# Two query groups and one key group change places in the hand-written order of an attention head loop

## The chip, the cores and the metric

The kernel runs on one core of a Trainium2 chip. The metric is the device time of one execution in microseconds (us). The core has five engines that run their own instruction streams in order and meet at semaphores: TensorE (PE, matmuls and transposes into PSUM), VectorE (DVE), ScalarE (ACT), GpSimd (POOL) and SyncE (SP, which issues DMAs). PE's clock is granted at one of two levels, 2.4 GHz (1.0 in the profile) or 1.2 GHz (0.5).

## The reference

A network of several layers on four images of 128 channels and 32 x 32 pixels: a non-local block and a mixture of convolutions, a causal attention, a feed-forward layer on the upper half of the tokens, an attention with three branches, and a mixture of experts. The change lies in the attention with three branches (16 heads of 64, 1024 tokens, batch 4). Cut to what matters:

```python
def _attn(q, k, v, mask=None):
    s = einsum('bhqd,bhkd->bhqk', q, k) / sqrt(64)
    return einsum('bhqk,bhkd->bhqd', softmax(where(mask, s, -1e9)), v)
o1 = _attn(q, k1, v1, causal)        # all earlier keys
o2 = _attn(q, ks, vs)                # 256 chosen tokens
o3 = _attn(q, kw, vw, winmask)       # the last 64 keys
o = g0 * o1 + g1 * o2 + g2 * o3      # gates, then a projection
```

q, ks and kw are each made of a plain half and a half that is rotated by position (rope).

## The kernel before, in words

stage_heads computes this attention in 16 passes (4 batches times 4 groups of 4 heads). Tokens are handled in groups of 256: the keys of the window are groups w0 to w3, the queries q0 to q3, the chosen keys s. Scores are computed twice: once with queries on partitions to find each query's maximum (near tiles for the window and the chosen keys, far tiles for all earlier keys), and once with keys on partitions, with the maxima subtracted in the same matmul, for the exponentials (score), the value products (value) and the denominators (add, sum). The numbers are kept in a high part rounded to fp32r and a low part, the rest.

A pass follows a list written out by hand, ORDER (L1971). Each engine walks through the whole list and does its share of each step. A step with a + belongs to the next pass and is done ahead, at the end of this one; the first such steps run once before the loop (the prologue, with clock-keeping matmuls between them), and the last pass has none. The steps that matter here:

- a.g: PE makes group g (L2388), ACT copies its plain half (L2572). rot.g: DVE multiplies the other half by the angles (L2656). rope.g: POOL adds the two products (L2327).
- tr.g: PE transposes the group with four transposes (L2398), ACT rounds it to its high part, with four copies for a query group and two for a key group (L2580). split.tr.g: DVE makes the low part with two instructions (L2674 for a query group, L2677 for a key group).
- near.i.n: PE makes a tile of scores of query tile i (L2430, and a mask at L2434 for the window keys), DVE takes its maxima (L2690). near.4.0 waits for split.tr.q2 and near.6.0 for split.tr.q3.
- v.x.n: PE makes values (L2416), ACT copies them (L2597). project.z: PE projects (L2517), DVE adds to the tokens (L2729).
- sum.z: PE makes denominators (L2510). norm.z: four DVE instructions in a row (L2714, L2716, L2718, L2722) turn, invert and apply them.
- double.w3: a DMA by SP, when tr.w3 is rounded. load.next: seven DMAs by SP for the next pass.

Two rules of the plan set most waits. The steps a, tr, k1, v, near and far ("filled" jobs, 97 in a pass) share PSUM banks 0 to 2, and each takes the next bank in the order of the list:

```python
self.bank = {key: n % 3 for n, (key, _) in enumerate(self.jobs)}
def bank_free(key, q):
    old = plan.before(plan.jobs, key, q, lambda other: plan.bank[other] == plan.bank[key])
    return old and (consumer[old[0]], ("split", *old) if old[0] in ("tr", "k1") else ("rot", old[1]) if old[0] == "a" else old)
```

plan.before finds the last job with the same bank, at need in the pass before. A job's matmuls thus wait for the last reader of that bank: the rotation of an a group, the split of a tr group or a key product, the copy of a v, the maxima of a near or far tile. The steps score, turn and sum share banks 3 to 5 in the same way.

At near.4.0 PE waits for its bank, issues nine matmuls whose result is overwritten (keep_clock(9, bank), L2426 and L2524), and only then waits for split.tr.q2.

Of the kernel before, what the change touches and what calls it, by code (L numbers as in the profile page):

```python
# [1968 lines left out]


ORDER = """  # L1971
wk tr.q2 tr.q3 split.tr.q2 split.tr.q3
score.4.0
score.4.1 v.v1.0 near.4.0
score.4.2
score.4.3
score.5.0 +load.next near.4.1 near.4.2 near.4.3
score.5.1 near.5.0
score.5.2
score.5.3 near.5.1 near.5.2 v.v1.1 near.5.3 near.6.0 value.4.4 near.6.1 near.6.2 near.6.3 turn.0.2 near.7.0 value.5.5 add.7 near.7.1 near.7.2 k1.0 near.7.3  # L1980
# [57 lines left out]
+score.1.1  # L2038
+score.2.0
+score.2.1  # L2040
+score.3.0 +rope.w3 +v.vw.1 +rope.q2 ysum.5 +v.vs.0 +tr.w3 +split.tr.w3 +a.q3 +rot.q3 +double.w3 project.5 +value.0.0 +value.1.1 +value.2.2 +add.0 +add.1 +value.3.3 +add.2 +add.3 +add.4 +add.5 +add.6 +sum.0 +rope.q3 +norm.0
"""


# [140 lines left out]
def stage_heads(nc, keep, PS, P, T, ident, identb, masks, turned, latents, d, slots, emptied):  # L2185
    with ExitStack() as ctx:
# [46 lines left out]
        def after(eng, q, at, *events):  # L2233


            values = {}
            for name, key in filter(None, events):
                value = plan.value(name, key, q, at)
                if value is not None:
                    values[name] = max(value, values.get(name, 0))  # L2240
            for name, value in values.items():
                eng.wait_ge(s[name], value if q is None else q * plan.a_pass(name) + value)
# [8 lines left out]
        def near_part(i, n):  # L2251

            if n < 2:
                return 1, KEEP3, 0
            return 2, 128 + REACH if i else 128, max(0, i * 128 - REACH)
# [5 lines left out]
        with nc.Block() as block:  # L2261
# [110 lines left out]
            def _(pe):  # L2372
# [4 lines that stand above are left out]
# [43 lines left out]
                def near_scores(key, q, at):  # L2420
                    _, i, n = key
                    made = {0: ("s", "w0", "q0"), 2: ("w1", "q1"), 4: ("q2",), 6: ("q3",)}[i] if n == 0 and i % 2 == 0 else ()
                    bank, x, w, c0 = ring(key), *near_part(i, n)
                    after(pe, q, at, bank_free(key, q))
                    if i == 4 and n == 0:
                        keep_clock(9, bank)  # L2426
                    after(pe, q, at, *(("reduced", ("split", "tr", g)) for g in made))
                    for m in range(2):
                        h = 2 * (n % 2) + m
                        last = nc.tensor.matmul(bank[:, m * w:(m + 1) * w], QH[:, h, i * 128:(i + 1) * 128], keys[x][:, h, c0:c0 + w],  # L2430
                                                start=m == 0, stop=x == 1 and m == 1)
                    if x == 2:
                        add = masks[:, 1:3, :].rearrange("p a n -> p (a n)")[:, 256 - w:]
                        last = nc.tensor.matmul(bank[:, 0:2 * w].rearrange("p (m w) -> p m w", m=2), identb[:, :],  # L2434
                                                add[:, None, :].broadcast_to([128, 2, w]), start=False, stop=True)
                    last.then_inc(s["filled"], 1)
# [84 lines left out]
                def keep_clock(count, bank=P[7]):  # L2521

                    for _ in range(count):
                        nc.tensor.matmul(bank[:, 0:384], identb[:, :], masks.rearrange("p a n -> p (a n)"), start=True, stop=True)  # L2524

                def one_pass(g, q):
                    for at, (ahead, *key) in enumerate(steps):
                        what, key = key[0], tuple(key)
                        if plan.left_out(q, ahead):
                            continue  # L2530
                        if q is None and what in ("a", "tr", "v", "near"):
                            keep_clock(2)
                        if what == "a":
                            group(key, q, at)
                        elif what == "tr":
                            turn_group(key, q, at)
                        elif what == "k1":
                            key_product(key, q, at)
                        elif what == "v":
                            value_product(key, q, at)  # L2540
                        elif what == "near":
                            near_scores(key, q, at)
                        elif what == "far":
                            far_scores(key, q, at)
                        elif what == "turn":
                            turn_maxima(key, q, at)
                        elif what == "score":
                            if q is None and key == ("score", 0, 0):
                                pe.wait_ge(s["rows"], 48)
                            key_major(key, q, at)  # L2550
                        elif what == "value":
                            values(key[1], key[2], q, at)
                        elif what == "sum":
                            denominators(key, q, at)
                        elif what == "project":
                            project(key[1], g, q, at)
# [327 lines left out]
```

## Time and profile before

| | us |
|---|---|
| three runs, median | 2646.47 |
| lowest, highest | 2644.33, 2648.10 |
| the profiled execution | 2643.02 |
| its span, first to last instruction | 2641.1 |

The head loop lies between 700 and 2400 us of the span. The profile is of one execution. Its page lists the busy time of each engine and the costliest groups of instructions; the trace behind it can be asked for a timeline of an engine, for the waits of an engine with what ended them, and for the busy time and the granted clock in any stretch. Times in a timeline are the start from the span's first instruction and the duration. Consecutive instructions of the same line and tiles are merged there into one row (x8: eight of them). The ends of matmuls are modelled, and a matmul may begin while the one ahead is still draining, so that starts are a better measure of PE than durations. What stands in brackets is the idle time of the engine before the row and what ended it.

### The profile page before, as it was taken

How to read it: one execution, taken by the hardware profiler on the slowest of the kernel's cores; microseconds unless marked ns; L12 is line 12 of the kernel's file. 1: busy time of each engine (PE TensorE's matmuls, PEld its weight loads, DVE VectorE, ACT ScalarE, POOL GpSimd, SP SyncE). 2: the span in 40 equal slices, each digit the busy share in tenths (PEclk: the TensorE clock that was granted, in tenths of full speed). 3: DMA queues.
4: the chain of work that ended last, by engine and by line, in shares of the span. 5: the costliest groups of instructions: out<-in, count | busy, mean ns of one | idle time of the engine just before them, and what ended most of it. 6: DMA issues, size and time to landing. Idle time of an engine off the chain costs nothing. (4 is left out here: it accounts for less than half of the span.)

```text
span 2641.1 us, 51557 instructions
## 1 busy us (share of the span) xinstructions
PE 2367.4 (90%) x16821; PEld 1718.4 (65%) x16821; DVE 1814.2 (69%) x3640; ACT 1413.0 (53%) x2489; POOL 1285.8 (49%) x972
## 2 busy tenths in 40 slices
PE   6889968666899999999999999999999999999767
PEld 4666645454667767677676676767667676675656
DVE  5868745585577686776867768676776867766436
ACT  2135544232565656656566565665657666575223
POOL 1016760000264746647365573755737557375445
PEclk8989988768999999999999999999999999999678
DMA  3040300013412111220212202122021220210233
GB/s 118 1 102 20 78 10 1 16 50 87 129 43 54 28 41 36 49 54 16 54 36 45 58 16 54 36 45 58 16 54 36 45 58 16 54 20 17 70 118 102
DMA packets 82189, 128.14 MB, mean 49 GB/s; under 512 B 15824, under 2 KB 58240, under 8 KB 81728
## 3 DMA queue, kind: packets, MB, share of 16 engines
q1 hardware_dynamic: 77616, 119.47, 17.9%
q0 software_dynamic: 3024, 7.43, 0.9%
q8 instruction: 46, 0.75, 0.1%
q10 hardware_dynamic: 1472, 0.24, 0.1%
q14 instruction: 31, 0.25, 0.0%
HBM read 61.26 MB, written 20.79 MB: 31 GB/s over the span
## 5 line engine op out<-in xcount | busy, mean ns | idle before, releaser
L2621 ACT ACTIVATE a_PT<-PS 128x512 f32<-128x512 f32 (+1 forms) x1104 | 584.4, 565 | 365.1 <-PE PS L2486 241.4
L2339 POOL TENSOR_TENSOR a_KT<-a_PT 128x256 f32<-128x256 f32 (+2 forms) x176 | 354.3, 2025 | 459.7 <-ACT a_PT L2621 451.2
L2339 POOL TENSOR_TENSOR a_KT<-a_KT,a_PT 128x2048 f32<-128x2048 f32 (+3 forms) x128 | 391.8, 3061 | 10.3 <-ACT a_PT L2621 1.0
L2690 DVE TENSOR_REDUCE a_NM<-PS 128x2 fp32r<-128x512 f32 (+2 forms) x512 | 290.8, 612 | 134.2 <-PE PS L2430 73.5
L2480 PE MATMUL PS<-a_QH,a_K 128*128 128x512 f32 (+3 forms) x768 | 293.1, 392 | 2.9 <-ACT a_PT L2621 2.8
L2702 DVE TENSOR_REDUCE a_MX<-PS 128x1 f32<-128x512 f32 (+3 forms) x432 | 265.6, 664 | 32.7 <-PE PS L2445 18.1
L2480 PE MATMUL PS<-a_QH,a_KSW 128*128 128x192 f32 (+3 forms) x832 | 264.5, 339 | 12.1 <-DVE a_NM L2690 10.5
L2445 PE MATMUL PS<-a_K,a_QH 128*128 128x512 f32 (+3 forms) x768 | 252.3, 404 | 9.4 <-DVE a_K L2677 8.1
L2481 PE MATMUL PS<-a_QL,a_K1B 76*128 76x512 f32 (+3 forms) x768 | 260.1, 349 | 0.0
L2430 PE MATMUL PS<-a_KSW,a_QH 128*128 128x256 f32 (+2 forms) x1024 | 198.8, 306 | 4.1 <-DVE a_QL L2674 4.1
L2430 PEld LDWEIGHTS PS<-a_KSW,a_QH 128*128 128x128 f32 x1024 | 164.0, 193 | 49.6 <-DVE a_NM L2690 19.5
L2327 POOL TENSOR_TENSOR a_TM<-a_R 128x128 f32<-128x128 f32 x288 | 124.1, 458 | 130.0 <-DVE a_R L2656 130.0
L2480 PEld LDWEIGHTS PS<-a_QH,a_KSW 128*128 128x128 f32 x832 | 160.4, 193 | 41.3 <-issue 13.5
L2677 DVE TENSOR_TENSOR a_KSW<-PS,a_KSW 64x512 fp32r<-64x512 f32 x160 | 110.3, 689 | 108.3 <-ACT a_KSW L2580 105.3
L2580 ACT ACTIVATE a_QH<-PS 64x512 fp32r<-64x512 f32 x256 | 151.5, 592 | 51.3 <-PE PS L2398 46.6
L2486 PE MATMUL PS<-masks,identb 128*128 128x128 bf16 (+3 forms) x592 | 172.2, 291 | 0.0
L2480 PEld LDWEIGHTS PS<-a_QH,a_K 128*128 128x128 f32 x768 | 149.0, 194 | 33.6 <-issue 14.5
L2445 PEld LDWEIGHTS PS<-a_K,a_QH 128*128 128x128 f32 x768 | 135.6, 193 | 45.5 <-DVE a_MX L2702 17.3
L2607 ACT ACTIVATE a_QL<-PS 12x1024 fp32r<-12x1024 f32 x128 | 130.1, 1017 | 60.7 <-PE PS L2460 58.3
L2481 PEld LDWEIGHTS PS<-a_QL,a_K1B 76*128 76x128 f32 x768 | 147.1, 192 | 9.6
L2656 DVE TENSOR_TENSOR a_R<-PS,a_angles 128x512 f32<-128x512 f32 x144 | 96.2, 687 | 72.9 <-ACT a_TM L2572 71.9
L2481 PE MATMUL PS<-a_QL,a_KWB 76*128 76x192 f32 (+2 forms) x576 | 141.1, 275 | 0.0
(434 smaller groups left out, 5223.2 us busy)
## 6 DMA issues: line engine op xcount, KB each, us to landing
a_KWB<-a_KSW SPq DMA_DIRECT2D x64, 256.0 KB, 3.3
a_K1B<-a_K SPq DMA_DIRECT2D x32, 512.0 KB, 4.9
a_XC<-latents SPq DMA_DIRECT2D x16, 512.0 KB, 3.8
a_CKS<-latents SPq DMA_DIRECT2D x16, 512.0 KB, 4.6
a_CF<-latents SPq DMA_DIRECT2D x16, 448.0 KB, 4.2
slots<-in_empty_slots SPq DMA_DIRECT2D x1, 5160.0 KB, 18.7
f_XB<-slots SPq DMA_DIRECT2D x8, 645.0 KB, 6.0
c_EX<-in_experts SPq DMA_DIRECT2D x1, 4608.0 KB, 18.0
```

The source lines that it names most:

```text
L2327: last = nc.gpsimd.tensor_tensor(TM[:, x, :, 32 + c:48 + c], r[:, :, 0, c:c + 16], r[:, :, 1, other:other + 16], ALU.add)
L2339: nc.gpsimd.tensor_tensor(total, one_in, other_in, ALU.add).then_inc(s["added"], 1)
L2430: last = nc.tensor.matmul(bank[:, m * w:(m + 1) * w], QH[:, h, i * 128:(i + 1) * 128], keys[x][:, h, c0:c0 + w], start=m == 0, stop=x == 1 ...
L2445: last = nc.tensor.matmul(bank[:, m * w:(m + 1) * w], QH[:, h0 + m, i * 128:(i + 1) * 128], K1[:, h0 + m, c0:c0 + w], start=m == 0, stop=n ...
L2480: nc.tensor.matmul(out, keys[x][:, h, c:c + 128], QH[:, h, start:start + w], start=m == 0, stop=False)
L2481: last = nc.tensor.matmul(out, upper[x][0:DH + ROWS, h, c:c + 128], QL[0:DH + ROWS, h, start:start + w], start=False, stop=mask is None an ...
L2486: last = nc.tensor.matmul(by_heads[:, :, 0:cols], identb[:, :], add[:, None, :].broadcast_to([128, each, cols]), start=False, stop=True)
L2580: last = nc.scalar.activation(odd_even({"q": QH, "w": KW, "s": KS}[g[0]], e, rows, tokens(g)), ring(key)[e * DH:(e + 1) * DH, :].rearrange ...
L2607: nc.scalar.activation(QL[DH:DH + ROWS, :, p * PAIR:(p + 1) * PAIR], turning(key)[DH:DH + ROWS, None, 0:PAIR].broadcast_to([ROWS, QUAD, PA ...
L2621: nc.scalar.activation(PT[:, to:to + width], turning(key)[:, 0:width], ACT.Exp).then_inc(s["taken"], 1)
L2690: nc.vector.tensor_reduce(NM[:, i, DH:].rearrange("p (h x) -> p h x", x=3)[:, h:h + 2, x], ring(key)[:, 0:2 * w].rearrange("p (h n) -> p h ...
L2702: nc.vector.tensor_reduce(out, ring(key)[:, 0:heads * w].rearrange("p (h n) -> p h n", h=heads), AX.X, ALU.max, negate=True).then_inc(s["r ...
```

## The change

tr.q3 with its split moves from the start of a pass to behind near.4.3. tr.q2 with its split moves from the start of a pass to the end of the pass before, ahead of tr.w3; project.5 moves ahead of both. split.tr.w3, rot.q3 and rope.q3 move behind norm.0, in this order. The nine clock-keeping matmuls at near.4.0 go.

```diff
 ORDER = """
-wk tr.q2 tr.q3 split.tr.q2 split.tr.q3
+wk
 score.4.0
 score.4.1 v.v1.0 near.4.0
 score.4.2
 score.4.3
-score.5.0 +load.next near.4.1 near.4.2 near.4.3
+score.5.0 +load.next near.4.1 near.4.2 near.4.3 tr.q3 split.tr.q3
 score.5.1 near.5.0
 score.5.2
 score.5.3 near.5.1 near.5.2 v.v1.1 near.5.3 near.6.0 value.4.4 ...
...
-+score.3.0 +rope.w3 +v.vw.1 +rope.q2 ysum.5 +v.vs.0 +tr.w3 +split.tr.w3 +a.q3 +rot.q3 +double.w3 project.5 +value.0.0 +value.1.1 +value.2.2 +add.0 +add.1 +value.3.3 +add.2 +add.3 +add.4 +add.5 +add.6 +sum.0 +rope.q3 +norm.0
++score.3.0 +rope.w3 +v.vw.1 +rope.q2 ysum.5 +v.vs.0 project.5 +tr.q2 +split.tr.q2 +tr.w3 +a.q3 +double.w3 +value.0.0 +value.1.1 +value.2.2 +add.0 +add.1 +value.3.3 +add.2 +add.3 +add.4 +add.5 +add.6 +sum.0 +norm.0 +split.tr.w3 +rot.q3 +rope.q3
...
                     after(pe, q, at, bank_free(key, q))
-                    if i == 4 and n == 0:
-                        keep_clock(9, bank)
                     after(pe, q, at, *(("reduced", ("split", "tr", g)) for g in made))
```

## Rows read from the trace of the kernel before

**Rows 1.** The page, busy time, share of the span and instructions of each engine

```profile
PE 2367.4 (90%) x16821; PEld 1718.4 (65%) x16821; DVE 1814.2 (69%) x3640; ACT 1413.0 (53%) x2489; POOL 1285.8 (49%) x972
```

**Rows 2.** Windows of two passes: length, busy time by engine (instructions), granted clock, DMA

```profile
927.02:1039.40 112.38, 108.75 (x793) 78.08 (x793) 80.67 (x136) 70.72 (x127) 65.22 (x50) 0.98 0.17 41
...
1482.29:1593.01 110.72, 107.16 (x793) 77.27 (x793) 80.65 (x136) 70.50 (x127) 65.20 (x50) 1.00 0.18 41
```

**Rows 3.** Waits of PE from 816 to 2380: total us, times, longest

```profile
PE PS L2524 <- DVE a_QL L2674: 24.7, 15, 1.7
```

**Rows 4.** Timeline of PE around the head of a pass: start, duration, line, tiles

```profile
1472.98 0.60 PE L2398 MATMUL PS<-ident,a_TM 128*128 128x128 f32 x4
1473.47 1.13 PE L2388 MATMUL PS<-a_WQ,a_CF 112*128 112x256 f32 x4
1474.44 1.05 PE L2517 MATMUL PS<-a_WP,a_YT 128*128 x8
...
1476.72 1.06 PE L2510 MATMUL PS<-a_KT,a_ones 128*32 128x512 f32 x8
1477.71 1.09 PE L2398 MATMUL PS<-ident,a_TM 128*128 128x128 f32 x8
1478.56 0.48 PE L2480 MATMUL PS<-a_QH,a_KSW 128*128 128x512 f32 x1
...
1479.58 1.06 PE L2416 MATMUL PS<-a_WV,a_CF 112*128 112x128 f32 x8
1482.29 1.64 PE L2524 MATMUL PS<-masks,identb 128*128 128x384 bf16 x9 [1.66 <-DVE a_QL L2674]
1483.63 0.54 PE L2430 MATMUL PS<-a_KSW,a_QH 128*128 128x256 f32 x2
...
1485.41 0.60 PE L2430 MATMUL PS<-a_KSW,a_QH 128*128 128x256 f32 x4
...
1486.28 0.53 PE L2480 MATMUL PS<-a_QH,a_KSW 128*128 128x512 f32 x1
...
1488.04 0.60 PE L2430 MATMUL PS<-a_KSW,a_QH 128*128 128x256 f32 x4
...
1488.66 1.06 PE L2416 MATMUL PS<-a_WV,a_CF 112*128 112x128 f32 x8
```

**Rows 5.** Timeline of DVE in the same stretch

```profile
1474.90 1.39 DVE L2677 TENSOR_TENSOR a_KSW<-PS,a_KSW 64x512 fp32r<-64x512 f32 x2 [4.58 <-ACT a_KSW L2580]
1476.32 0.69 DVE L2656 TENSOR_TENSOR a_R<-PS,a_angles 128x512 f32<-128x512 f32 x1
...
1477.93 0.72 DVE L2714 STREAM_TRANSPOSE a_RT<-PS 128x512 f32<-128x512 f32 x1 [0.33 <-PE PS L2510]
...
1479.81 0.69 DVE L2722 TENSOR_TENSOR a_YA<-PS,a_RT 128x512 f32<-128x512 f32 x1
...
1480.85 1.39 DVE L2674 SCALAR_TENSOR_TENSOR a_QL<-PS,a_QH 64x512 fp32r<-64x512 f32 x2
...
1485.85 2.22 DVE L2690 TENSOR_REDUCE a_NM<-PS 128x2 fp32r<-128x512 f32 x4 [0.47 <-PE PS L2430]
```

**Rows 6.** Timeline of ACT in the same stretch

```profile
1478.41 4.83 ACT L2580 ACTIVATE a_QH<-PS 64x512 fp32r<-64x512 f32 x8 [2.83 <-PE PS L2398]
```

**Rows 7.** Timeline of POOL in the same stretch

```profile
1470.56 1.27 POOL L2348 TENSOR_TENSOR a_YT<-a_YA,a_YB 128x512 f32<-128x512 f32 x1 [2.51 <-DVE a_YB L2722]
```

**Rows 8.** Windows of two long idle times of PE in earlier stages and behind them

```profile
264.67:267.78 3.11, 0.00 (x1) 0.01 (x1) 3.11 (x5) 0.60 (x1) 2.82 (x3) 1.00 0.92 207
267.78:271.20 3.42, 3.42 (x17) 3.19 (x17) 1.37 (x4) 1.89 (x4) 2.17 (x2) 0.57 0.88 200
...
448.46:452.73 4.27, 0.00 (x1) 0.00 (x1) 3.08 (x23) 1.30 (x3) 0.00 (x0) 0.99 0.00 0
...
452.73:459.40 6.67, 6.67 (x41) 4.27 (x42) 3.77 (x9) 2.25 (x3) 0.00 (x0) 0.50 0.00 0
```

**Rows 9.** Timeline of PE at the start of the loop's first pass

```profile
700.83 0.43 PE L2398 MATMUL PS<-ident,a_TM 128*128 128x128 f32 x2 [2.77 <-DMA a_WP<-in_w_proj]
```

## The prediction

> **What bounds the kernel now.** The page comes first: TensorE (PE) is busy for 90% of the span, the next engine for 69% [rows 1]. The windows of single passes come next: a pass of the head loop, from one filler burst to the next, is 110.72 us, and PE is busy in 107.16 of them at full clock [rows 2]. The loop runs 16 passes. PE sets the pass, so each microsecond added to PE's order or taken from it counts 15 times, and once more, differently, in the first pass. The waits of PE over the loop say what is left to win: the longest, 24.7 us in 15 waits, is for the low parts that VectorE (DVE) makes at L2674 [rows 3], and the timeline shows where: nine fillers start at 1482.29 after 1.66 us of idling, and near.4.0 follows at 1483.63 [rows 4]. The spot that the change rewrites thus costs 1.66 + 1.34 = 3.0 us of a pass. Behind it PE runs without a gap as far as these rows go; a PE that comes out of this spot later is not given the time back.
>
> **The bank ring, which decides this.** Every "filled" job (a, tr, k1, v, near, far) takes the next of three PSUM banks in the order of the text, and its matmuls wait until the reader of the bank's last job is done. A pass has 97 such jobs, 3 x 32 + 1, so the first job of a pass takes the same bank as the last job of the pass before. Before, the first is tr.q2 and the last a.q3, whose reader rot.q3 is long done: DVE runs it at 1476.32 and PE needs it at 1477.71 [rows 4, 5]. After, the first is v.v1.0 and the last still a.q3, so v.v1.0 waits for rot.q3, and the change puts rot.q3 on DVE behind norm.0 and split.tr.w3. Counting on: near.4.0 gets tr.q2's bank, near.4.1 tr.w3's, tr.q3 near.4.1's, near.5.2 tr.q3's, v.v1.1 near.5.0's.
>
> **Part 1: the end of a pass on PE.** Times are those of the pass shown, in us past 1400. From tr.w3 (72.98) to sum.0 (76.72) PE does tr.w3, a.q3, project.5 and four value products [rows 4]. After, the same work stands there in another order, with tr.q2 added: 0.49 (one tr group, 72.98 to 73.47). sum.0 starts at 77.21 and, 0.99 long as before (76.72 to 77.71), gives way to score.4.0 at 78.20, where that had 78.56, since both groups are gone from there. project.5 can go first: its input is ready at 71.83 (70.56 + 1.27 on POOL [rows 7]). It is 1.05 long, so tr.q2 starts at about 74.0. PE wants v.v1.0 1.02 after score.4.0 (78.56 to 79.58), at 79.22.
>
> **Part 2: the same stretch on ScalarE (ACT) and DVE.** A q group is rounded by four copies; eight take 4.83, so four 2.42 and the two of tr.w3 1.2; they start 0.70 after the transposes (77.71 to 78.41) [rows 4, 6]. ACT rounds tr.q2 from 74.7 to 77.1 and tr.w3 to 78.3. DVE runs split.tr.q2 (1.39) to 78.5. norm.0 can start 1.21 after sum.0 (76.72 to 77.93), at 78.42, so it starts at 78.5 and takes 2.57 (77.93 to 79.81 + 0.69): 81.07. Then split.tr.w3, 1.39, and rot.q3, 0.69: 83.1 [rows 5]. PE goes on 0.05 after such a release (80.85 + 1.39 to 82.29): v.v1.0 at 83.15. **That is a wait of 3.9 us**, some 3.8 of it idle. v.v1.0 is 1.06 long, of which some 0.9 pass before the next job starts, so near.4.0, whose split is done long before, starts at about 84.0 where it had 83.63. The old wait and the fillers are gone, a longer wait has come: +0.4 in all.
>
> **Part 3: tr.q3 in its new place.** From near.4.0 to near.4.1 are 1.78 (83.63 to 85.41), then three near tiles take 0.87 (to 86.28) [rows 4]: PE is ready for tr.q3 at 86.65. Its bank is free when DVE has reduced near.4.1, which starts 0.44 after that tile does (85.41 to 85.85) and takes about 0.7 [rows 4, 5]: PE at 86.95, another 0.3. rope.q3, which DVE's rot.q3 releases at 83.1, has 3.5 us for two instructions on a POOL with nothing else to do. With 0.5 for tr.q3 itself score.5.1 starts at 87.45 where it had 86.28. Then ACT rounds q3 from 87.65 to 90.05, with the exponentials of score.5.1 to 5.3 queued behind, and DVE splits it to 91.45, with the maxima of near.5.0 and 5.1 queued behind. PE has near.5.1 at 89.2 (1.76 after score.5.1, 86.28 to 88.04) and would have near.5.2 some 0.25 later, but its bank is tr.q3's: 91.5. **A second wait, 2.1 us, some 1.9 idle.** v.v1.1 then waits for the maximum of near.5.0, 0.7 behind the split: 92.15 where it had 88.66. That is **+3.5 us a pass**; from there the order is as before.
>
> **Part 4: the clock.** In most passes PE stays at 2.4 GHz after the 1.66 us wait. In the one from 927.02 the grant falls, 0.98 in the mean, and it takes 112.38 instead of 110.72 [rows 2]: a fall costs 1.66 us. It is one of two such passes; the other 13 of those 15 waits leave the clock alone. Longer idling does not: after 3.11 us the grant was 0.57 over 3.42 us, after 4.27 us 0.50 over 6.67 us with PE busy throughout [rows 8]. 3.8 us lies between these two. I take a fall in nearly each pass at 1.5 us (1.66, less a part of the slow stretch that lies under the wait), bounds 0 and 3.0, the latter half of 6.67 less the end that the second wait hides. The second wait, 1.9 us idle, is nearest to the 1.66 us ones; between 2 in 15 there and every time at 3.11, I take 4 in 10 at 1.5: 0.6 a pass, bounds 0 and 1.66.
> The Trainium skill (TensorE: Matmul & The Clock Gate, section "A second HAM failure mode: psum-queue depth-cycling") speaks more strongly against such an order: it says that a PE which idles briefly between groups of matmuls as it cycles through PSUM banks keeps dropping to the slow clock and back. By that rule both waits would end in a fall in every pass, rival 2's time instead of the sum below; 13 of the 15 waits of 1.66 us do not bear it out.
>
> **What costs nothing.** double.w3 is issued when tr.w3 is rounded, 78.3, some 3.4 us later than now (ACT releases split.tr.w3 for 74.90 [rows 5]); the first score that reads it, score.7.0, has all of the near tiles 5 to 7 and four key products ahead of it. SP's seven loads for the next pass stand behind double.w3 in its queue; nothing reads them before a.s, behind score.13.1, half a pass on. Without that cover a pass would lose those 3.4 us. tr.q2's copies overwrite what score.24 read last, which PE issues ahead of tr.q2. score.4.2 needs norm.0's first transpose only, done at 79.2.
>
> **The first pass.** The load of WP stands on SP behind double.w3, and PE waits 2.77 us for WP, until 700.83 [rows 9]. q2's four copies now go ahead of tr.w3's on ACT, 2.4 us, and WP lands that much later. In return most of v.v1.0's wait passes under that one. With the 3.1 us of part 3 this pass loses about 3 us (0 to 6).
>
> **The sum**, against the profiled execution (2643.02 us; span 2641.1): 15 x 3.5 = 52.5, the first pass 3, the two falls of before gone -3.3, new falls 15 x (1.5 + 0.6) = 31.5, in all +83.7, so 2726.7 or **2727 us**. The median of the runs shown is 3.4 above the profiled one; the sum does not move for that.
>
> **Rivals.**
> 1. No low clock after either wait: 2643.0 + 52.5 + 3 - 3.3 = 2695. For it: 13 of 15 waits of before; against it: the rows at 3.11 and 4.27 us. 0.08.
> 2. Both waits end in a fall every time: 15 x (3.5 + 3.32) + 3 - 3.3 = 102, so 2745; with the first slow stretch twice as long 15 x (3.5 + 3.0 + 0.6) + 3 - 3.3 = 106, 2749. For it: the long idle rows; against it: 13 of 15. 0.10.
> 3. Not slower: rot.q3 is not what v.v1.0 waits for in the end. The point is 79.22: with rot.q3 done by then v.v1.0 goes at once, near.4.0 at 80.1, and near.4.1, held by split.tr.w3 (82.4), at 82.45, 3.3 sooner than in my sum (85.8). All behind it moves along: 3.5 - 3.3 = 0.2 a pass, and 2643.0 + 3 + 3 - 3.3 = 2646, no change. For it: the 3.0 us of wait and fillers do go. Against it: the ring as counted, and a DVE chain of 2.57 + 1.39 + 0.69 behind sum.0 with 1.0 us of PE work beside it. 0.05.
> 4. Faster: as 3, with split.tr.w3 and q3's rounding hidden too. Then the 3.0 us come out in full: 2643 - 45 = 2598. ACT and DVE would have to do 2.42 + 1.39 beside the 2.5 us that PE has from tr.q3 to near.5.2. 0.04.
> The forecast keeps 0.73. A measurement of this kernel can tell about 0.2%, 5 us, from no change. Faster 0.04, same 0.05, slower 0.91. The range goes from rival 1 to rival 2 with some room: 2692 to 2752.
>
> **What would show it.** No fillers at near.4.0. PE waiting at the value product (L2416) for DVE's rotation (L2656), some 3.8 us, 15 times; PE waiting at a near tile (L2430) for L2674, some 1.9 us, 15 times. Passes of 114.2 us at full clock, 116 to 117 with falls, and a granted clock clearly below 1.00 over the loop. The forecast is wrong if v.v1.0 starts within 1 us of score.4.1's end, or if near.5.2 does not wait.

## The result, and the profile after

The changed kernel takes 2753.12 us (median of four runs, 2752.69 to 2754.90) where the kernel before takes 2645.65 beside it (2644.33 to 2648.10): a ratio of 1.0411, 95% interval 1.0397 to 1.0425, slower by 4.1%. The forecast was 2727 in 2692 to 2752: the right sign and the right waits, 26 us too little, and the time lies 1 us above the range. Behind the removed lines the line numbers fall by two: the wait for L2674 of before is one for L2672 here, the rotation is L2654.

The page of after, busy time, share and instructions of each engine (against [rows 1]): PE has 39 us more of busy time with 142 matmuls fewer, so its matmuls became slower.

```profile
PE 2406.6 (87%) x16679; PEld 1741.3 (63%) x16679; DVE 1816.6 (66%) x3640; ACT 1419.2 (52%) x2489; POOL 1286.2 (47%) x972
```

Waits of PE in the loop of after, 820 to 2490 us: total, times, longest (against [rows 3]). The one wait of 1.7 us has become three.

```profile
PE PS L2416 <- DVE a_R L2654: 48.9, 15, 3.3
PE PS L2428 <- DVE a_QL L2672: 30.6, 15, 2.0
...
PE PS L2478 <- DVE a_RT L2712: 7.1, 14, 0.5
```

Windows of after: a pass from score.4.0 to score.4.0, four stretches of it, and the pass behind it: length, busy time by engine (instructions), granted clock, DMA (against [rows 2]). From the fourth pass on, passes of 118.5 and 117.1 us alternate; the second kind lacks the second slow stretch. In the stretches from 1528.13 and from 1541.78 PE runs at 1.2 GHz.

```profile
1524.38:1642.84 118.46, 110.57 (x788) 79.10 (x784) 80.78 (x137) 70.95 (x127) 65.26 (x50) 0.96 0.17 39
...
1524.38:1528.13 3.75, 1.46 (x8) 0.60 (x4) 3.49 (x6) 2.10 (x5) 0.00 (x0) 1.00 0.56 134
1528.13:1534.95 6.82, 5.34 (x19) 4.76 (x20) 2.40 (x4) 1.97 (x4) 0.97 (x2) 0.50 0.48 126
1534.95:1541.78 6.83, 4.68 (x29) 3.70 (x29) 4.34 (x8) 4.46 (x8) 1.03 (x1) 1.00 0.00 0
1541.78:1545.19 3.41, 3.41 (x19) 1.98 (x17) 1.57 (x3) 0.69 (x1) 3.41 (x1) 0.50 0.00 0
...
1642.84:1759.94 117.10, 109.25 (x788) 78.67 (x784) 80.93 (x137) 70.95 (x127) 65.31 (x50) 0.97 0.17 39
```

Timeline of PE in after at the head of that pass: start, duration, line, tiles, and in brackets the idle time before and what ended it (against [rows 4]). sum.0, score.4.0, score.4.1, v.v1.0, near.4.0, near.4.1, tr.q3, near.5.2, v.v1.1:

```profile
1523.41 1.04 PE L2508 MATMUL PS<-a_KT,a_ones 128*32 128x512 f32 x8
1524.38 0.50 PE L2478 MATMUL PS<-a_QH,a_KSW 128*128 128x512 f32 x1
...
1525.62 0.50 PE L2478 MATMUL PS<-a_QH,a_KSW 128*128 128x512 f32 x1 [0.51 <-DVE a_RT L2712]
...
1529.61 2.08 PE L2416 MATMUL PS<-a_WV,a_CF 112*128 112x128 f32 x8 [3.27 <-DVE a_R L2654]
1531.34 0.78 PE L2428 MATMUL PS<-a_KSW,a_QH 128*128 128x256 f32 x2
...
1534.47 0.82 PE L2428 MATMUL PS<-a_KSW,a_QH 128*128 128x256 f32 x4
...
1535.88 0.66 PE L2398 MATMUL PS<-ident,a_TM 128*128 128x128 f32 x4
...
1540.46 0.47 PE L2428 MATMUL PS<-a_KSW,a_QH 128*128 128x192 f32 x2 [2.04 <-DVE a_QL L2672]
...
1541.18 1.56 PE L2416 MATMUL PS<-a_WV,a_CF 112*128 112x128 f32 x8
```

Timeline of DVE in after (against [rows 5]): split.tr.q2, norm.0's first and last instruction, split.tr.w3, rot.q3, one behind the other without a gap, as counted beforehand:

```profile
1523.43 1.39 DVE L2672 SCALAR_TENSOR_TENSOR a_QL<-PS,a_QH 64x512 fp32r<-64x512 f32 x2 [2.04 <-ACT a_QH L2578]
1524.85 0.72 DVE L2712 STREAM_TRANSPOSE a_RT<-PS 128x512 f32<-128x512 f32 x1
...
1526.72 0.69 DVE L2720 TENSOR_TENSOR a_YA<-PS,a_RT 128x512 f32<-128x512 f32 x1
1527.44 1.39 DVE L2675 TENSOR_TENSOR a_KSW<-PS,a_KSW 64x512 fp32r<-64x512 f32 x2
1528.87 0.69 DVE L2654 TENSOR_TENSOR a_R<-PS,a_angles 128x512 f32<-128x512 f32 x1
```

Timeline of PE in after, the first pass (against [rows 9]): the wait for WP is 3.93 us and ends at 703.06, 2.2 later than before.

```profile
703.06 0.79 PE L2478 MATMUL PS<-a_QH,a_KSW 128*128 128x512 f32 x1 [3.93 <-DMA a_WP<-in_w_proj]
```

### The profile page after: what moved, and what is told of

It reads as the page before. It is cut to its first block and busy times, and to the rows that moved or that the text cites. A ratio compares the mean times of both kernels' runs of the same rounds, so it can differ in the third digit from the quotient of the medians.

```text
span 2750.6 us, 51259 instructions
## 1 busy us (share of the span) xinstructions
PE 2406.6 (87%) x16679; PEld 1741.3 (63%) x16679; DVE 1816.6 (66%) x3640; ACT 1419.2 (52%) x2489; POOL 1286.2 (47%) x972
## 5 line engine op out<-in xcount | busy, mean ns | idle before, releaser
L2478 PE MATMUL PS<-a_QH,a_KSW 128*128 128x192 f32 (+3 forms) x832 | 276.4, 353 | 23.7 <-DVE a_NM L2688 10.5
L2428 PE MATMUL PS<-a_KSW,a_QH 128*128 128x256 f32 (+2 forms) x1024 | 218.5, 326 | 36.7 <-DVE a_QL L2672 36.7
L2428 PEld LDWEIGHTS PS<-a_KSW,a_QH 128*128 128x128 f32 x1024 | 180.5, 212 | 90.9 <-DVE a_QL L2672 40.7
L2478 PEld LDWEIGHTS PS<-a_QH,a_KSW 128*128 128x128 f32 x832 | 166.5, 200 | 73.9 <-issue 30.9
L2654 DVE TENSOR_TENSOR a_R<-PS,a_angles 128x512 f32<-128x512 f32 x144 | 96.3, 687 | 72.9 <-ACT a_TM L2570 71.9
L2672 DVE SCALAR_TENSOR_TENSOR a_QL<-PS,a_QH 64x512 fp32r<-64x512 f32 x128 | 87.9, 687 | 80.6 <-ACT a_QH L2578 78.7
```

What stands on the lines that cost most here:

```text
L2478: nc.tensor.matmul(out, keys[x][:, h, c:c + 128], QH[:, h, start:start + w], start=m == 0, stop=False)
```

## The experiments

What is told apart is how much of the loss is the order alone and how much the clock, which part of the order makes the first wait, and what the removed matmuls had been doing. All kernels compute the whole result. Ratios are to the kernel before, run beside each; the "theory" of an expectation is what was held when it was written, and it changes on the way.

**The order with the clock held.** Fillers go into both waits, to banks whose readers are done.

```diff
+                    if (kind, x) == ("v1", 0):
+                        after(pe, q, at, bank_free(("near", 4, 0), q))
+                        keep_clock(18, ring(("near", 4, 0)))
...
+                    if (i, n) == (5, 2):
+                        after(pe, q, at, ("residual", ("project", 5)))
+                        keep_clock(11)
```

> The changed kernel with clock-keeping matmuls placed inside its two new waits: 18 ahead of v.v1.0, into the bank that near.4.0 overwrites afterwards, and 11 ahead of near.5.2, into the bank that value.4.4 overwrites. At 0.15 us each they take 2.7 and 1.65 us, less than the waits, so the order of the work and the waits stay. If the two waits cost 3.5 us a pass at full speed and all the rest of the loss is TensorE's clock, the grant stays near 1.00, passes take 114.2 to 115 us, and the kernel takes about 2643 + 15 x 3.5 + 3 = 2700 us (2695 to 2712). If the waits themselves cost 7 us a pass and the low clock falls into idle time, it stays at 2745 to 2755.

2703.89 us, ratio 1.0225 (1.0208 to 1.0242). Behind the first its passes are all alike, at full clock; the window of one:

```profile
1506.48:1620.90 114.42, 111.25 (x814) 78.79 (x812) 80.80 (x137) 70.85 (x127) 65.30 (x50) 1.00 0.17 40
```

What is left of the two waits that were filled (waits of PE, 820 to 2440 us):

```profile
PE PS L2419 <- DVE a_R L2660: 4.8, 15, 0.4
PE PS L2434 <- DVE a_QL L2678: 3.6, 15, 0.2
```

So the order costs 114.42 - 110.72 = 3.7 us a pass (3.5 in the forecast), and over half of the loss. The rest, 1.0411 against 1.0225, is the clock: 49 us where the forecast had 31.5.

**Only the first wait held.** The same without the eleven fillers at near.5.2.

> The changed kernel with the 18 clock-keeping matmuls ahead of v.v1.0 alone; the second wait, at near.5.2, idles as in the change. The order alone cost 60 us with both waits filled (2704). Theory (each wait's own idle time decides, and some 2 us at near.5.2 fell in 5 to 6 of 16 passes where tr.q3 alone was moved): 2704 + 6 x 1.6 = 2714 (2706 to 2720), so that the first wait's falls are worth some 40 of the 49 us that the clock cost, 2.6 each. Rival (with no low stretch behind the first wait, the second falls every time): 2704 + 15 x 1.6 = 2728 or more.

2727.94 us, ratio 1.0324 (1.0307 to 1.0342): the rival. One pass of it, and the slow stretch in it; the grant falls in each of the 15 passes behind the first one, after an idle time of 2.0 us:

```profile
1515.20:1631.18 115.98, 111.05 (x803) 78.56 (x801) 80.81 (x137) 70.87 (x127) 65.22 (x50) 0.99 0.17 40
1529.79:1533.20 3.41, 3.41 (x18) 1.78 (x16) 1.47 (x3) 0.69 (x1) 3.39 (x1) 0.50 0.00 0
```

A fall here costs 115.98 - 114.42 = 1.56 us a pass. In after the grant falls at this wait in 9 of the 15 passes only (from the fourth on in every second). Holding the first wait thus takes one slow stretch away and brings the other into every pass, and the 25 us between the two kernels are less than the first stretch is worth: passes of 117.1 with that stretch alone stand 2.7 above 114.42, and the second stretch adds 1.35 where it comes.

**norm.0 last.** split.tr.w3, rot.q3 and rope.q3 ahead of norm.0, the rest as in after.

```diff
-... +sum.0 +norm.0 +split.tr.w3 +rot.q3 +rope.q3
+... +sum.0 +split.tr.w3 +rot.q3 +rope.q3 +norm.0
```

> The changed kernel with norm.0 put back behind split.tr.w3, rot.q3 and rope.q3 (that part of the change undone). Theory, the chain norm.0, split.tr.w3, rot.q3 on VectorE holds v.v1.0: rot.q3 is done 2.6 us sooner, but score.4.1 now waits for the first transpose of norm.0, behind them, some 2.6 us, so v.v1.0 comes about 1.3 us sooner than in the changed kernel, and the clock still falls: 2753 - 15 x 1.3 = 2733 us (2715 to 2740). Rival, the order on VectorE is not what holds TensorE: 2753.

2726.13 us, ratio 1.0306 (1.0289 to 1.0323), as expected. The profile is of the longest of its five executions, 2739.41. Waits of PE, 820 to 2450 us:

```profile
PE PS L2478 <- DVE a_RT L2712: 35.4, 14, 2.5
PE PS L2428 <- DVE a_QL L2672: 28.6, 14, 2.0
```

v.v1.0 no longer waits for the rotation; in its place score.4.1 waits 2.53 us for norm.0. Which of the two stands last on DVE chooses who waits, and it changes the size: 2.53 us of idling for 3.78, and the slow stretch behind it is 3.41 us long in each of the 15 passes behind the first, where in after it is 6.83 in 14 of 15. The window of one such stretch:

```profile
1530.75:1534.16 3.41, 3.41 (x13) 2.94 (x12) 1.71 (x3) 1.81 (x4) 0.00 (x0) 0.50 0.68 223
```

**Another bank for v.v1.0.** The ring is shifted by one bank for the jobs at the head of a pass, so that v.v1.0 takes the bank of tr.q2 and not of a.q3.

```diff
-        self.bank = {key: n % 3 for n, (key, _) in enumerate(self.jobs)}
+        self.bank = {key: (n + (n < 78)) % 3 for n, (key, _) in enumerate(self.jobs)}
```

> The changed kernel with the bank ring turned by one for the first 78 jobs of a pass, so that v.v1.0 takes the bank of tr.q2 in place of that of a.q3; nothing else. Theory, the bank of a.q3 makes the first wait: TensorE no longer waits for the rotation at v.v1.0; near.4.0, which now has the bank of tr.w3, waits for split.tr.w3 instead, 1.7 us, and starts 1.6 us sooner than in the changed kernel. Idle times are then below 2.1 us and the clock falls in fewer passes: 2643 + 15 x (3.5 - 1.6) + 3 = 2675 at full clock, 2675 to 2705 with falls. Rival, the ring does not matter: 2753.

2720.69 us, ratio 1.0298 (1.0271 to 1.0326): the wait for the rotation is gone, which shows that the bank had made it, but the time is 16 us above the expected range. Waits of PE, 820 to 2450 us:

```profile
PE PS L2428 <- DVE a_QL L2672: 30.1, 15, 2.1
PE PS L2428 <- DVE a_KSW L2675: 24.6, 15, 1.7
```

The window of a pass:

```profile
1512.81:1626.92 114.11, 107.82 (x785) 77.50 (x783) 80.88 (x137) 70.94 (x127) 65.32 (x50) 0.99 0.17 40
```

near.4.0 now waits 1.7 us for split.tr.w3, about as long as it had in [rows 3], and yet one or two slow stretches fall in every pass (114.1 to 116.6 us). That spoke against the reading that 1.66 us of idling leaves the clock alone, and led to the kernel without fillers, below.

**tr.q3 alone.** The kernel before, nine fillers kept, with tr.q3 and its split behind near.4.3.

```diff
-wk tr.q2 tr.q3 split.tr.q2 split.tr.q3
+wk tr.q2 split.tr.q2
...
-score.5.0 +load.next near.4.1 near.4.2 near.4.3
+score.5.0 +load.next near.4.1 near.4.2 near.4.3 tr.q3 split.tr.q3
```

> The kernel before with tr.q3 and its split moved behind near.4.3 and nothing else changed (fillers kept). The fillers then stand in a bank that is free, so they run inside the wait for split.tr.q2 and near.4.0 starts some 1.3 us sooner; tr.q3 in its new place costs 0.8 us and the wait at near.5.2 and v.v1.1 2.7 us. Theory: +2.2 us a pass, 2643 + 33 = 2676 us, and up to 2690 if the clock falls behind the second wait in half of the passes. Rival, tr.q3's place costs nothing and the loss all comes from the first wait: 2625, faster than before.

2682.97 us, ratio 1.0156 (1.0134 to 1.0177), as expected. Two passes, without and with a fall, which comes behind the 2.0 us wait at near.5.2 (in 6 of the 15 passes behind the first):

```profile
1495.22:1607.92 112.70, 108.09 (x794) 77.17 (x793) 80.70 (x136) 70.60 (x126) 65.22 (x51) 1.00 0.18 41
1946.02:2060.23 114.21, 109.59 (x794) 77.78 (x793) 80.69 (x137) 70.59 (x126) 65.25 (x51) 0.99 0.17 40
```

This part of the change alone costs 2.0 us a pass at full clock. That is a net figure: with tr.q3 gone from the ring ahead of it, near.4.0's bank is free sooner, the fillers run inside the first wait, and near.4.0 comes 4.17 us behind score.4.0 where it came 5.07 behind it in before.

**Before without its fillers.**

```diff
-                    if i == 4 and n == 0:
-                        keep_clock(9, bank)
```

> The kernel before without its nine clock-keeping matmuls at near.4.0, nothing else. They stand behind PE's wait for its bank and end 1.34 us behind the release by split.tr.q2 (1482.29 to 1483.63 in the trace of before), so without them near.4.0 starts 1.34 us sooner; part of this is given back at score.4.3, which needs a bank whose exponential ACT has not done by then. Theory (the clock follows the idle time, and 1.66 to 2.0 us of it leave the grant alone in most passes): passes of about 110.2 us, a fall in a third of them at most, 2632 to 2645. Rival (the fillers are what keeps the clock at full speed): the grant falls in every pass, 15 x 1.66 = 25 us more, 2655 to 2670.

2658.56 us (2644.70 to 2671.23), ratio 1.0054 (1.0024 to 1.0085): the theory that held up to here fell. Three passes:

```profile
1599.15:1711.79 112.64, 109.00 (x785) 78.70 (x784) 80.98 (x136) 70.54 (x126) 65.15 (x51) 0.97 0.18 41
1937.10:2047.39 110.29, 105.97 (x785) 76.22 (x784) 80.68 (x137) 70.39 (x126) 65.22 (x51) 1.00 0.18 42
2047.39:2159.22 111.83, 107.48 (x785) 77.49 (x784) 80.97 (x136) 70.40 (x126) 65.21 (x51) 0.98 0.18 41
```

At full clock the order is indeed worth 0.43 us a pass (110.72 to 110.29). But the grant falls in 12 of 15 passes, in eight of them for twice as long as in the others, against 2 of 15 with the fillers, behind the same idle time of 1.7 us. So the nine matmuls that followed that idle time in before did matter. One long fall and one short one, near.4.0 and the slow stretch of each, and a fall of before:

```profile
1603.59 0.77 PE L2428 MATMUL PS<-a_KSW,a_QH 128*128 128x256 f32 x2 [1.70 <-DVE a_QL L2672]
1603.50:1610.33 6.83, 6.74 (x21) 5.48 (x22) 3.88 (x6) 4.54 (x9) 0.00 (x0) 0.50 0.00 0
...
2051.83 0.47 PE L2428 MATMUL PS<-a_KSW,a_QH 128*128 128x256 f32 x2 [1.75 <-DVE a_QL L2672]
2054.06:2057.47 3.41, 3.41 (x14) 2.94 (x13) 2.55 (x5) 1.78 (x4) 0.00 (x0) 0.50 0.00 0
...
927.06:930.47 3.41, 3.41 (x12) 2.07 (x13) 1.38 (x2) 2.56 (x5) 0.00 (x0) 0.50 0.00 0
```

The fillers are no plain guard against a fall, though. In the eight long ones the slow stretch starts within 0.1 us of the wait's end, and in both falls of before close to it too (0.04 and 0.11 us behind it): with the nine fillers it lasts 3.41 us, without them 6.83. In the other four it starts 1.9 to 2.7 us behind the wait's end, and before has no fall of that kind. The eight follow one another, each in a pass of 112.6 to 112.7 us, so the 12 are not 12 separate chances. A pass without fillers is also 0.43 us shorter at full clock; whether that alone moves the falls was not tried.

**Before with its fillers inside the wait.** Eleven to bank 7 ahead of the wait, in place of nine behind it.

```diff
                     if i == 4 and n == 0:
+                        after(pe, q, at, ("residual", ("project", 5)))
+                        keep_clock(11)
+                    after(pe, q, at, bank_free(key, q))
-                        keep_clock(9, bank)
```

> The kernel before with its clock-keeping matmuls put into the wait instead of behind it: eleven of them go to bank 7, free since project.5, ahead of PE's wait for split.tr.q2 at near.4.0, in place of the nine behind that wait. Theory (what holds the clock is that PE works during the 1.66 us, and the 1.34 us behind the wait are then saved): passes of 110.3 us as without fillers, and no fall, 2643 - 15 x 0.42 - 3.3 = 2633 (2628 to 2640). Rival (the fillers hold the clock only behind the wait): falls as in e4_no_fillers, 2650 to 2665.

2634.73 us, ratio 0.9963 (0.9948 to 0.9979), as expected. The window of a pass:

```profile
1472.33:1582.58 110.25, 107.72 (x796) 77.20 (x795) 80.69 (x136) 70.42 (x126) 65.17 (x51) 1.00 0.18 42
```

PE's timeline at near.4.0, the fillers and the near tile:

```profile
1474.86 1.95 PE L2525 MATMUL PS<-masks,identb 128*128 128x384 bf16 x11
1476.77 0.48 PE L2431 MATMUL PS<-a_KSW,a_QH 128*128 128x256 f32 x2
```

No pass but the first has a slow stretch, and near.4.0 follows the fillers at once. Placed in the wait, fillers cost nothing; placed behind it, they held near.4.0 up by 1.34 us. Part of that is made up at score.4.3, where PE waits 0.58 us without the delay, and 0.47 us a pass is left (110.72 to 110.25).

**The next pass's work in DVE's idle time.** An order that follows from this: tr.q2 with its split, v.v1.0, the near.4 tiles and near.5.0 of the next pass at the end of a pass, where DVE idled 4.58 us [rows 5]; sum.0 and norm.0 to the head, behind score.4.1; tr.q3 behind near.5.2; no fillers.

```diff
-wk tr.q2 tr.q3 split.tr.q2 split.tr.q3
 score.4.0
-score.4.1 v.v1.0 near.4.0
-score.4.2
+score.4.1 near.5.1 near.5.2 tr.q3 sum.0 norm.0
+score.4.2 split.tr.q3 near.5.3
...
+score.21.3 +near.1.2 +rope.w2 +tr.w2 +rope.q1 +wk +double.w1 ...
...
++score.2.1 +split.tr.q2 +rot.q3
++score.3.0 +split.tr.w3 ysum.5 +near.4.0 project.5 +v.vs.0 +near.4.1 +near.4.2 ...
```

> An order of my own that follows from the diagnosis: no clock-keeping matmuls; tr.q2 with its split, v.v1.0, the four near.4 tiles and near.5.0 of the next pass stand at the end of a pass, where DVE idles 4.58 us ahead of split.tr.w3 in the kernel before; sum.0 and norm.0 move behind score.4.1, tr.q3 behind near.5.2, so that no wait of PE has norm.0, a split and a rotation in a row ahead of it. Theory (the 1.66 us wait and the 1.34 us of fillers both leave the path, and no new wait comes for the low parts of q2): 15 x 3.0 to 15 x 3.9 us less, 2585 to 2605, PE without a wait over 1 us for L2674's line. Rival (the wait only moves, to the rounding of tr.q2 and tr.w3 at the pass's end or to the split of q3 at near.6.0): 2640 or more.

2653.42 us (2631.66 to 2665.22), ratio 1.0037 (1.0010 to 1.0064): the gain did not come. The waits at the head are gone, but PE waits 1.70 us elsewhere, at near.2.0, and in the profiled execution, one of 2644.95, the grant falls there in 8 of 15 passes. PE's timeline at near.2.0:

```profile
1565.78 0.74 PE L2427 MATMUL PS<-a_KSW,a_QH 128*128 128x256 f32 x4 [1.70 <-DVE a_QL L2671]
```

DVE's timeline, the subtraction of wk ahead of it:

```profile
1559.16 2.65 DVE L2679 TENSOR_TENSOR a_WKL<-a_WK,a_WKH 64x256 fp32r<-64x256 f32 x1 [1.41 <-ACT a_WKH L2599]
```

POOL's timeline, the addition that runs at that time:

```profile
1556.98 4.55 POOL L2338 TENSOR_TENSOR a_KT<-a_KT,a_PT 128x2048 f32<-128x2048 f32 x1
```

The subtraction of wk takes 2.65 us here, 0.41 in before, and it ends 0.28 after the addition that POOL had begun ahead of it (1559.16 + 2.65 = 1561.81, against 1556.98 + 4.55 = 1561.53). The split of q1, which near.2.0 needs, stands behind it.

**wk beside an idle POOL.** The same order with wk behind split.tr.q3.

```diff
-score.4.2 split.tr.q3 near.5.3
+score.4.2 split.tr.q3 wk near.5.3
...
-score.21.3 +near.1.2 +rope.w2 +tr.w2 +rope.q1 +wk +double.w1 ...
+score.21.3 +near.1.2 +rope.w2 +tr.w2 +rope.q1 +double.w1 ...
```

> The order of e6_ahead with one step put elsewhere: wk (the split of the key projection's weight into a high and a low part) goes from behind rope.q1, near the end of a pass, to behind split.tr.q3. In e6_ahead its subtraction on DVE, with both inputs in SBUF, took 2.65 us there, beside POOL additions that follow one another without a gap (4 in 17.44 us), against 0.41 us in the kernel before beside an idle POOL; the split of q1 stood behind it and PE waited 1.70 us for that at near.2.0, 15 times. Theory (POOL's running addition holds the subtraction up): it takes 0.4 us again, no wait over 0.8 us is left in the loop, the clock does not fall, passes of 108.0 us, 2600 (2592 to 2612). Rival (the length comes from elsewhere, or the wait goes to another place): passes of 109.5 us or more, 2625 to 2655.

2595.42 us, ratio 0.9821 (0.9787 to 0.9856): the theory, and 1.8% faster than the kernel before. The two longest waits of PE, 820 to 2360 us:

```profile
PE PS L2477 <- DVE a_NM L2687: 9.8, 15, 0.7
PE PS L2442 <- DVE a_K L2674: 7.4, 15, 0.5
```

The window of a pass:

```profile
1459.39:1567.17 107.78, 106.41 (x784) 76.11 (x784) 80.79 (x137) 70.05 (x127) 65.21 (x50) 1.00 0.18 42
```

DVE's timeline, the subtraction of wk:

```profile
1463.18 0.41 DVE L2679 TENSOR_TENSOR a_WKL<-a_WK,a_WKH 64x256 fp32r<-64x256 f32 x1
```

No wait of PE over 0.7 us is left in the loop, no slow stretch either, and a pass is 2.94 us shorter than in [rows 2], about the 3.0 us that the wait and the fillers had cost there.

## Why the prediction was right in kind and short in size

- **The bank ring held.** v.v1.0 waits for rot.q3 in all 15 passes, 3.27 us, and 0.51 at score.4.1 ahead of it makes 3.78, where 3.8 was forecast. Moving one bank removes that wait. The 0.51 was not foreseen: the forecast let only score.4.2 depend on norm.0's first transpose, and it is score.4.1. It cost nothing, since it lies inside the time to rot.q3.
- **Parts 1 and 2 held.** From score.4.0 to v.v1.0 are 5.23 us (1524.38 to 1529.61); the forecast had 4.95. near.4.0 then follows after 1.73, not 0.9, for the clock is already low.
- **Part 3 held.** near.5.2 idles 2.04 us (1.9 forecast), and the order costs 3.7 us a pass at full clock (3.5).
- **Part 4 failed, in the term of the first fall.** It took 1.5 us a pass, with 3.0 as its upper bound. The slow stretch is 6.82 us, of which 1.5 lie under the wait and PE works 5.34 [the window from 1528.13]; work at half speed loses half of that, 2.67 us, and the passes with this stretch alone are 2.7 longer. The idle time, 3.8 us, lay between the two rows of [rows 8], whose slow stretches are 3.42 and 6.67 us, and the forecast took its price from the pass at 927.02, where a wait of 1.66 us was followed by a stretch of 3.41. That is 1.2 us in 15 passes, 18 of the 26 us.
- **The second fall was right in the mean by luck.** 1.35 us in about every second pass is some 0.7; the forecast had 4 in 10 at 1.5, 0.6. But its row, 13 of 15 waits of 1.66 us that left the clock alone, said nothing of a wait without fillers: take them away and 12 of 15 fall. The sum that put the fillers down as 1.34 us of pure cost, and the use of 13 of 15 against rival 2, both fall with it: taking the fillers out alone won 0.43 us a pass at full clock and lost more than that to the clock.
- **The first pass** starts 1.4 us later (703.06 for 701.67) and lasts 114.34 for 110.91: 4.8 in all, 3 forecast (0 to 6). With 0.2 a pass in part 3, 3 us, 1 us in the second falls, and some 2 us from the last pass's start to the end of the span (275.2 us in before, 284.1 in after: 8.9 more, where the sum had 5.6), this fills the remaining 8 us.
- **Rivals.** 1 (no fall) is what holding the clock by force gives, 2704 for 2695. 2 came nearest: its variant with the first stretch twice as long, 2749, priced that stretch at 3.0 and left the second at 0.6; both waits falling every time did not come. The Trainium skill (TensorE: Matmul & The Clock Gate, section "A second HAM failure mode: psum-queue depth-cycling") says that PE's short idling between groups of matmuls, as it cycles through PSUM banks, makes the clock swing between its two levels. The trace agrees with it here for the first wait, 15 of 15, and for the second once the first is held, 15 of 15. For the second wait in after itself it is 9 of 15. 3 and 4 did not come: v.v1.0 does wait for rot.q3.
- **What was put at nothing was nothing:** no wait of PE for double.w3 or for a load of the next pass is among the waits of the loop.

What stays open is why the grant falls at near.5.2 in every pass of one order, in 9 of 15 of another and in 6 of 15 of a third, at the same 2.0 us of idling, and why a slow stretch is 3.41 us long in one case and 6.83 in another. The runs show only that the length of the idle time does not settle it, and that matmuls in or behind a wait matter. A count such as 6 of 15 is that of one execution, and falls came in rows (eight passes on end in the kernel without fillers); it is no chance that carries over to another order.

## What to carry to other kernels

Before moving a step in a hand-ordered stream, count the ring of buffers through the wrap (97 jobs on 3 banks), and read what stands ahead of each bank's last reader on its own queue. Clock-keeping matmuls are not a cost to be struck out without a price: in a bottleneck engine's wait they were free here, behind it they cost part of their length (0.47 of 1.34 us), and without them waits of 1.6 to 2.1 us were followed by a fall in 6 to 15 of 15 passes. Move work into an engine's idle time only after looking at what the engine that shares its memory access is doing there.

## What the runs showed of the hardware

- A wait of 1.7 us at near.4.0 was followed by a fall to 1.2 GHz in 2 of 15 passes with nine matmuls behind it and in 12 of 15 without; with eleven matmuls inside the wait there was no fall behind the first pass. A stretch that began at the wait's end lasted 3.41 us with the nine behind it, 6.83 without.
- The slow stretches shown from after last 6.82 and 3.41 us; in the shorter one PE is at 1.2 GHz while busy throughout.
- A DVE subtraction with both inputs in SBUF took 2.65 us beside a running POOL addition and 0.41 beside an idle POOL. The Trainium skill (SBUF — State Buffer, section "SBUF: two separate sides") says that DVE and GpSimd share a port pair as a lock, held for a whole instruction, also against a DVE instruction with two SBUF inputs, where the GpSimd instruction reads SBUF. The trace agrees within what the spans on POOL can tell: both of POOL's inputs lie in SBUF, and the end came 0.28 us after the addition's, against the 0.41 us that the subtraction takes alone. That moving one such instruction would cost 2.2 us of DVE time, and through one wait and its slow stretches 58 us of the kernel (2653.42 to 2595.42), had not been expected.
